# One tile for the B, c and sb rows, and the first chunk's down products ahead of the row-tile session

## What is computed

```
gate = x @ W_gate.T + 0.5 * (x @ A_gate[id].T) @ B_gate[id].T     # up: the same with its own weights
act  = silu(gate) * up                                            # 1376 columns
down = act @ W_down.T + 0.5 * (act @ A_down[id].T) @ B_down[id].T
x    = x + down @ sign(W0).T + bias0
y    = (x @ B1[id1].T) @ A1[id1].T
x    = x + y @ (W1 + 2 * sum_n w_n B_n A_n).T + bias1
```

## Time and profile before

| what | value |
|---|---|
| median of 3 runs | 875.0 us (874.68 to 875.05) |
| the profiled execution's own time | 874.75 us |
| its span | 872.9 us |
| TensorE matmuls busy | 867.7 us (99% of the span) |
| TensorE weight loads busy | 714.2 us (82%) |
| VectorE busy | 523.2 us (60%) |
| ScalarE busy | 231.5 us (27%) |
| data moved by DMA | 205.60 MB, mean 236 GB/s |
| B rows, L437 | 128 transfers, 236.0 KB each, median 3.2 us to landing |

### The profile page before, as it was taken

One profiled execution on the slowest core, in us unless ns is written; L12 is line 12 of the kernel. 1 busy time (PEld: TensorE's weight loads), 2 busy tenths in 40 slices (PEclk: granted clock), 3 DMA queues, 4 the chain that ended last, 5 costly groups with the idle time before them and its releaser, 6 DMA issues.

```text
span 872.9 us, 21554 instructions
## 1 busy us (share of the span) xinstructions
PE 867.7 (99%) x7474; PEld 714.2 (82%) x7474; DVE 523.2 (60%) x1204; ACT 231.5 (27%) x460; POOL 86.8 (10%) x122
## 2 busy tenths in 40 slices
PE   9999999999999999999999999999999999999998
PEld 6888888888888888888888888888888888888885
DVE  5797556655555566556556665655656565656654
ACT  4953212222222122212222231212122222212210
POOL 0232000000010000100000000000000000000011
PEclk9999999999999999999999999999999999999999
DMA  9967788685877767587876757688675768868563
GB/s 347 408 229 267 228 253 262 195 268 163 257 250 237 249 219 239 180 257 227 256 247 227 245 178 248 208 268 256 223 238 184 245 198 264 265 217 266 190 173 89
DMA packets 159771, 205.60 MB, mean 236 GB/s; under 512 B 56064, under 2 KB 121600, under 8 KB 152064
## 3 DMA queue, kind: packets, MB, share of 16 engines
q1 hardware_dynamic: 101536, 117.14, 43.1%
q10 hardware_dynamic: 56096, 80.76, 27.8%
q0 software_dynamic: 2112, 7.34, 2.2%
HBM read 158.76 MB, written 15.20 MB: 199 GB/s over the span
## 4 chain that ended last, share of the span: by engine, by line
PE 99%; DVE 1%; ACT 0%; issue 0%; DVEq 0%
PE gu_ps L1125 56%; PE y_ps L1230 27%; PE out_ps L1252 3%; PE gu_ps L1340 3%; PE out_ps L1303 2%; PE gu_ps L1331 1%; PE out_ps L1239 1%; PE y_ps L1125 1%; PE out_ps L1125 1%; PE gu_ps L1230 1%; PE out_ps L1260 1%; PE gu_ps L1424 0%; DVE a_lo L817 0%; PE gu_ps L1380 0%; DVE weff_raw L1032 0%; PE y_ps L1307 0%
## 5 line engine op out<-in xcount | busy, mean ns | idle before, releaser
L1230 PE MATMUL y_ps<-down_sb,actT_sb 128*128 128x512 f32 x1023 | 241.5, 393 | 0.0
L1230 PEld LDWEIGHTS y_ps<-down_sb,actT_sb 128*128 128x128 f32 x1023 | 189.6, 188 | 60.3 <-issue 21.4
L1125 PE MATMUL gu_ps<-wg_sb,xT_sb 128*128 128x432 f32 x768 | 164.0, 362 | 0.5 <-DVE act_all L835 0.5
L1125 PE MATMUL gu_ps<-wu_sb,xT_sb 128*128 128x432 f32 x768 | 160.8, 358 | 0.0
L1125 PEld LDWEIGHTS gu_ps<-wu_sb,xT_sb 128*128 128x128 f32 x768 | 144.5, 188 | 8.3
L1125 PEld LDWEIGHTS gu_ps<-wg_sb,xT_sb 128*128 128x128 f32 x768 | 141.7, 188 | 11.6 <-DVE xT_sb L817 1.4
L591 ACT CAST actT_sb<-landed 128x512 fp32r<-128x512 f32 (+1 forms) x96 | 51.1, 585 | 162.1 <-DMA landed<-act_all 89.4
L537 POOL TENSOR_TENSOR b_two<-b_raw,const_sb 128x128 f32<-128x128 f32 x62 | 24.2, 411 | 685.4 <-DMA b_raw<-in_b1tab 685.4
L1125 PE MATMUL gu_ps<-slot,s_sb 128*128 128x512 f32 x270 | 66.8, 392 | 0.0
L839 DVE STREAM_TRANSPOSE act_all<-act_all 128x512 f32<-128x512 f32 (+1 forms) x96 | 64.1, 668 | 3.3
L591 ACT COPY ad_two<-a_raw 128x352 f32<-128x352 f32 x64 | 28.0, 485 | 126.2 <-PE out_ps L1252 125.5
(11 more groups left out here) (173 smaller groups left out, 929.9 us busy)
## 6 DMA issues: line engine op xcount, KB each, us to landing
slot<-t_table ACTq DMA_DIRECT2D x59, 1024.0 KB, 8.0
b_rows<-in_btab SPq DMA_DIRECT2D x128, 236.0 KB, 3.2
a_raw<-in_atab SPq DMA_DIRECT2D x128, 152.0 KB, 8.0
landed<-act_all SPq DMA_DIRECT2D x132, 64.0 KB, 4.7
xT_raw<-in_xT SPq DMA_DIRECT2D x32, 256.0 KB, 2.6
x_in<-in_x SPq DMA_DIRECT2D x32, 256.0 KB, 10.3
landed<-act_all ACTq DMA_DIRECT2D x124, 64.0 KB, 4.7
out_x<-out_sb SPq DMA_DIRECT2D x31, 256.0 KB, 8.3
```

The lines of the kernel that those rows point to most:

```text
L1125: last = nc.tensor.matmul(o, w, m, start=start and n == 0, stop=stop and n == len(terms) - 1, skip_group_check=not check)
L1230: last = nc.tensor.matmul(to[:], actT_sb[:, ACTT_SLOT[c] + n, a, :], down_sb[:, blk, b, :], start=begin and (c, n) == (0, 0) and (a, b) == ...
```

## The change

It does four things. The tiles `b_rows` and `cs_rows` become one, `rows_sb` (2 x 944): columns 0 to 511 of groups 2 and 3 take the c and sb rows, columns 512 to 943 chunk 2's B rows. The table of B is cut in two: `btab` holds 944 columns for groups 0 and 1, `btab2` 432 columns for groups 2 and 3, and the load of a step has eight transfers in place of four, 32 partitions each (118 KB and 54 KB by their shapes). TensorE's wait for `x1_done` and `down` for chunk 0 stand ahead of the session, so `down` opens `y_ps` and the down rows add to it. The c rows of the last step get a tile `c_end` of their own, and four small tiles of the prologue get places of their own.

```diff
-                    rows, n = rows_of(b, 0, 4)
-                    sp.dma_start(b_rows[rows, n, :],
-                                 btab[bass.ds(at[b], P), :].rearrange("(q r e) w -> q r (e w)", q=4, e=2)
+                    rows, n = rows_of(b, 0, 2)
+                    sp.dma_start(rows_sb[rows, n, :],
+                                 btab[bass.ds(at[b], P), :].rearrange("(q r e) w -> q r (e w)", q=2, e=4)
+                                 ).then_inc(L["b_in"], 16)
+                for b in range(GB):
+                    rows, n = rows_of(b, 2, 4)
+                    sp.dma_start(rows_sb[rows, n, H:PAIR],
+                                 btab2[bass.ds(at[b], P), :].rearrange("(q r e) w -> q r (e w)", q=2, e=4)
                                  ).then_inc(L["b_in"], 16)
...
-            def down_rows(n, to=y_ps, begin=True):
-                return nc.tensor.matmul(to[pair(n), :], lhs_sb[group(3), pair(n)], cs_rows[group(3), n, :],
-                                        start=begin, stop=False, skip_group_check=True)
+            def down_rows(n, to=y_ps):
+                return nc.tensor.matmul(to[pair(n), :], lhs_sb[group(3), pair(n)], rows_sb[group(3), n, 0:H],
+                                        start=False, stop=False, skip_group_check=True)
...
                 if prev is not None:
                     pe.wait_ge(L["td_ready"], g)
                     pe.wait_ge(L["sbd_in"], 16 * GB * g)
-                    after(pe, L["x1_done"], prev)
...
                 gate(g, 2)
                 up(g, 2)
+                if prev is not None:
+                    after(pe, L["x1_done"], prev)
+                    down(prev, 0, begin=True).then_inc(L["y_mm"], 1)
                 lora_ready(g, j, parity, prev, pp)
                 first_rows(prev, pp)
                 second_rows()
                 if prev is not None:
-                    for c in range(NC):
+                    for c in range(1, NC):
                         down(prev, c).then_inc(L["y_mm"], 1)
```

More of the change, by code:

```diff
@@ L141, in build_adaln_ffn @@
         lhs2_sb = place("lhs2_sb", [P, P], f32)
-        rows_at = [cursor[0]]
-        b_rows = place("b_rows", [P, PAIRS, PAIR], f32)
-        cs_rows = place("cs_rows", [P, PAIRS, H], f32)
+        rows_sb = place("rows_sb", [P, PAIRS, PAIR], f32)
         rows_end = cursor[0]
@@ L178, in build_adaln_ffn @@
         const_sb = place("const_sb", [P, CONST_W], f32, line=32)
+        c_end = nc.alloc_sbuf_tensor_at("c_end", [P, PAIRS, H], f32, offset=s0_at)
+        assert s0_at + 4 * PAIRS * H <= pair_end
         b1_end = nc.alloc_sbuf_tensor_at("b1_end", [P, PAIRS, KC, 2, RANK], f32, offset=a_at)
         idx_feat = place("idx_feat", [P, 2, BATCH], i32, line=32)
+        bias0_sb = nc.alloc_sbuf_tensor_at("bias0_sb", [P, H], f32, offset=cursor[0])
+        id_raw = place("id_raw", [P, 2, BATCH], i32, line=32)
+        id_f = place("id_f", [P, 2, BATCH], f32, line=32)
+        idle_sb = nc.alloc_sbuf_tensor_at("idle_sb", [P, 512], bf16, offset=cursor[0])
+        cursor[0] += 1024
         assert cursor[0] <= nc.sbuf_usable_end, (cursor[0], nc.sbuf_usable_end)
@@ L369, in load_sbd, with load_c @@
                 rows, n = low_rows(b, 3)
-                engine.dma_start(cs_rows[rows, n, :], sb_view[bass.ds(at[b], P), :].rearrange("(r e) w -> r (e w)", e=8)
+                engine.dma_start(rows_sb[rows, n, 0:H], sb_view[bass.ds(at[b], P), :].rearrange("(r e) w -> r (e w)", e=8)
                                  ).then_inc(L["sbd_in"], 16)
-        def load_c(engine, at, batch=range(GB), to=2, signal=L["c_in"]):
+        def load_c(engine, at, batch=range(GB), to=rows_sb, r=2, signal=L["c_in"]):
             for b in batch:
-                rows, n = low_rows(b, to)
-                engine.dma_start(cs_rows[rows, n, :], c_view[bass.ds(at[b], P), :].rearrange("(r e) w -> r (e w)", e=8)
+                rows, n = low_rows(b, r)
+                engine.dma_start(to[rows, n, 0:H], c_view[bass.ds(at[b], P), :].rearrange("(r e) w -> r (e w)", e=8)
                                  ).then_inc(signal, 16)
@@ L475, in step @@
                 else:
-                    load_c(sp, table_rows(SP, 1, g), range(GB), 1, E["c_in"])
+                    load_c(sp, table_rows(SP, 1, g), range(GB), c_end, 1, E["c_in"])
                 if prev is not None:
@@ L1300, in small, with out_rows @@
                 last.then_inc(L["small_mm"], 1)
-            def out_rows(n, r=2, to=out_ps, at=slice(0, H)):
-                return nc.tensor.matmul(to[pair(n), at], lhs_sb[group(r), pair(n)], cs_rows[group(r), n, at],
+            def out_rows(n, r=2, rows=rows_sb, to=out_ps, at=slice(0, H)):
+                return nc.tensor.matmul(to[pair(n), at], lhs_sb[group(r), pair(n)], rows[group(r), n, at],
                                         start=True, stop=True, skip_group_check=True)
-            def down_rows(n, to=y_ps, begin=True):
-                return nc.tensor.matmul(to[pair(n), :], lhs_sb[group(3), pair(n)], cs_rows[group(3), n, :],
-                                        start=begin, stop=False, skip_group_check=True)
+            def down_rows(n, to=y_ps):
+                return nc.tensor.matmul(to[pair(n), :], lhs_sb[group(3), pair(n)], rows_sb[group(3), n, 0:H],
+                                        start=False, stop=False, skip_group_check=True)
             def lora_ready(g, j, parity, prev, pp):
@@ L1331, in first_rows @@
                         last = nc.tensor.matmul(gu_ps[GU_BANK[0][u]][pair(n), 0:w], lhs_sb[group(u), pair(n)],
-                                                b_rows[group(u), n, 0:w], start=False, stop=True, skip_group_check=True)
+                                                rows_sb[group(u), n, 0:w], start=False, stop=True, skip_group_check=True)
                 last.then_inc(L["first_mm"], 1)
@@ L1338, in second_rows @@
                         c, u = 1 + r // 2, r % 2
-                        lhs, w = lhs_sb if c == 1 else lhs2_sb, CHUNKS[c][1]
+                        lhs, at, w = (lhs_sb, B_SECOND, MID) if c == 1 else (lhs2_sb, H, CHUNKS[2][1])
                         last = nc.tensor.matmul(gu_ps[GU_BANK[c][u]][pair(n), 0:w], lhs[group(r), pair(n)],
-                                                b_rows[group(r), n, B_SECOND:B_SECOND + w], start=False, stop=True,
+                                                rows_sb[group(r), n, at:at + w], start=False, stop=True,
                                                 skip_group_check=True)
@@ L1396, in finish @@
                 for n in range(PAIRS):
-                    last = down_rows(n, y_end, False)
+                    last = down_rows(n, y_end)
                 last.then_inc(L["y_mm"], 1)
@@ L1417, in finish @@
                     for n in range(PAIRS):
-                        last = out_rows(n, 1, bank, columns(half))
+                        last = out_rows(n, 1, c_end, bank, columns(half))
                     last.then_inc(L["first_mm"], 1)
@@ L1512 @@
     wd[:, used] = v["L0_cond_W_down"][:, order.reshape(FP)[used]]
-    b_rows = np.zeros((R0, 4, RANK, PAIR), np.float32)
-    for u, part in enumerate((gate_b, up_b)):
-        part = part.reshape(R0, RANK, F)
-        for c, (f, w) in enumerate(CHUNKS):
-            to = 0 if c == 0 else B_SECOND
-            b_rows[:, u + (2 if c == 2 else 0), :, to:to + w] = part[:, :, f:f + w]
+    by_row = [part.reshape(R0, RANK, F) for part in (gate_b, up_b)]
+    wide, narrow = (np.stack([np.concatenate([part[:, :, CHUNKS[c][0]:sum(CHUNKS[c])] for c in cs], axis=2) for part in by_row],
+                             axis=1) for cs in ((0, 1), (2,)))
     b1_rows = v["L1_cond_B"][:, :, turned_features(0, H, KC).reshape(H)].reshape(R1, RANK, KC, P)
@@ L1528 @@
         "bd": feat(v["L0_cond_B_down"][0].transpose(1, 0, 2).reshape(H, R0 * RANK)),
-        "btab": b_rows.reshape(R0 * P, PAIR // 2),
+        "btab": wide.reshape(R0 * P, PAIR // 4),
+        "btab2": narrow.reshape(R0 * P, CHUNKS[2][1] // 4),
         "atab": np.concatenate([a_rows, ad_rows], axis=1),
```

9 lines of the change are left out of this document (3 added, 6 removed).

## The result

The changed kernel takes 877.26 us in the median of 17 executions (875.65 to 878.05), the kernel before 875.0 us in 17 on the same chip (874.68 to 875.32). The ratio is 1.0023, with an interval of 1.0017 to 1.003: 2.3 us slower, or 0.23%. The forecast was 876.1 us. The profiled execution took 876.61 us (span 874.8 us), 1.9 us over the profiled one of before.

The account below looks back on a forecast made before the run. TensorE, busy 706.00 of 706.00 us from 126 to 832 us, bounds the loop; the last step's chain leaves it. Terms 0 + 0 + 1.1 + 0 = +1.1 us gave a median of 876.1 us, range 873.9 to 879.0.

Parts of the forecast that it names:

- A: The forecast case: only the last step's tail pays, 876.1 us, within 875.4 to 877.0; chance 0.60.
- the mark for slower: Whole kernel: a median over 876.75 us counts as slower, since measurement resolves 0.2% (1.75 us); chance 0.23.
- B: Rival: in most loop pairs later act sends meet weight-table loads, making p3 or `small` late; 880.3 us with the tail; chance 0.12.
- E: Rival: B rows come late, serialized, costing 0.3 us in each odd step; 880.3 us; chance 0.04.
- The move costs nothing on TensorE: Around the session: the same 9 down matmuls run, 2.08 us, before it and not after; 0 us.
- rival D: Session entry gets cheaper, its waits met under 512-column matmuls: 0.08 us in each of 31 sessions, 873.6 us; chance 0.12.
- 2.08 us later behind the session, hidden 30 times: Work following the session shifts every step but stays covered in the loop: 0 us, at most 0.2; not hidden the 31st time.
- The B rows cost nothing: Each step's B load: eight issues fit SyncE's queue and rows land before their session; 0 us.
- E's 3.4 us of spare: SyncE's queue: slack claimed after the last B row issue before the session needs the rows, making late rows unlikely.
- The tail, +1.1 us: Last step: chunk 0's low part delays add_y and down of chunk 1; +1.1 us, bounds 0 and 2.08.
- The step that failed: Last step's end: `low_rank_rows` follows down of chunk 1 and x1's landing, moved 1.04 us; the chain behind keeps 1.1.

Follow-up runs that it names:

- fillers: Changed kernel plus five filler matmuls in TensorE's gap of the last step, between the down products of steps 30 and 31: 877.6 us, ratio 1.0023.
- last two steps: Kernel before, with chunk 0's down products ahead of the session in steps 30 and 31 only: 876.18 us, ratio 1.0012.
- two chunks ahead: Kernel before, with chunks 0 and 1 of down (21 matmuls) ahead of the session in step 31 only: 881.26 us, ratio 1.0072.
- The swap: Changed kernel, with ScalarE's two sends of x1 put ahead of its two sb row loads in the last step: 876.43 us, ratio 1.0017.
- the move alone: Kernel before, with chunk 0's nine down matmuls ahead of the session, old tiles and four B transfers kept: 876.56 us, ratio 1.0024.
- the tables alone: Changed kernel with its tiles and split tables, but down wholly behind the session as before: 875.03 us, ratio 1.0003.
- step 31 alone: Kernel before, with chunk 0's nine down matmuls ahead of the session only in the last step: 875.82 us, ratio 1.0012.

## Why the spare of x1 was gone

ScalarE and its queue in the last step: before, changed, and changed with fillers (the long execution); of each the cast of chunk 1, the sb rows and the sends of x1.

```profile
855.26 0.62 ACT L591 CAST actT_sb<-landed 128x512 fp32r<-128x512 f32 x1 [0.93 <-DMA landed<-act_all]
855.81 0.88 ACTq L370 DMA_DIRECT2D cs_rows<-sb_table  x2
857.42 1.47 ACTq L350 DMA_DIRECT2D x_landed<-x_turn  x2
```

```profile
858.25 0.62 ACT L598 CAST actT_sb<-landed 128x512 fp32r<-128x512 f32 x1 [1.07 <-DMA landed<-act_all]
858.71 0.80 ACTq L372 DMA_DIRECT2D rows_sb<-sb_table  x2
859.55 1.36 ACTq L352 DMA_DIRECT2D x_landed<-x_turn  x2
```

```profile
857.98 0.62 ACT L598 CAST actT_sb<-landed 128x512 fp32r<-128x512 f32 x1 [1.33 <-DMA landed<-act_all]
858.58 1.01 ACTq L372 DMA_DIRECT2D rows_sb<-sb_table  x2
859.63 1.45 ACTq L352 DMA_DIRECT2D x_landed<-x_turn  x2
```

Before, the queue is idle from 856.69 to 857.42 and waits for the transpose of x1. After the change it is never idle: the sends follow the sb rows at once (859.51, 859.55), since the cast of chunk 1 ahead of them moved by 2.99 us and the transpose by 1.72 (0.99 us of both had been lost before the last session). From the end of these sends to `low_rank_rows`' turn on TensorE (the end of the matmuls ahead of it) it is 861.03 - 858.89 = 2.14 us before, 862.92 - 860.91 = 2.01 after, and 857.39 + 5.00 - 861.08 = 1.31 in the long execution. In the first two the last of these sends lands 0.5 to 0.6 us before that turn, in the third 1.2 us after it.

The 0.7 us between 2.01 and 1.31 would by themselves have made it late by 0.2 us. The other 1.0 us is the landing, which takes longer there. These are the second send of x1 on ScalarE's queue and the load of x on SyncE's, in the low and in the long execution:

```profile
860.14 0.77 ACTq L352 DMA_DIRECT2D x_landed<-x_turn  x1
860.65 0.59 SPq L465 DMA_DIRECT2D x_in<-in_x  x1
```

```profile
860.19 0.60 SPq L465 DMA_DIRECT2D x_in<-in_x  x1
860.29 0.79 ACTq L352 DMA_DIRECT2D x_landed<-x_turn  x1
```

In the low one the send (64 KB) is issued 0.5 us ahead of the load (256 KB) and lands in 2.26 us; in the long one it is issued 0.1 us behind the load and takes 3.30 us, and lands 0.3 us after the load does. All 14 profiles split this way: in 11 the send goes first, by 0.18 to 0.95 us, and takes 2.14 to 2.40 us; in three (fillers, last two steps, two chunks ahead) it goes 0.1 us behind, and takes 3.30 to 3.36. So a send that is late by a few tenths lands a whole us later, which fits an upper and a lower group of executions. No run moved the load of x to test this.

The few tenths come from chunk 1. Its cast starts 9.07 to 9.19 us behind the first matmul of the last session in those three profiles, and 8.68 to 8.90 in the others, but for two: that with chunk 0's sends shared, which has another order, and that with the old order in the last step. There it starts 9.22 us behind, as late as in the long ones, and the sends of x1 go out right behind the transpose all the same.

So the transfer had only some 0.5 us of spare before the change either. What the change took away is the idle time in front of its sends, which had absorbed a late chunk 1.

## The prediction, point by point

- *The time.* The forecast was +1.1 us and +2.3 came. 877.26 us is over 877.0, the upper end of what A allows, and over 876.75, the mark for slower, which had 0.23. It lies within 873.9 to 879.0 because that range reached up for B and E, whose waits in the loop did not come. That part is luck.
- *The move costs nothing on TensorE.* Right: 11.85 us from `up` to the next `gate` in both. The session's entry did not become cheaper (rival D), its idle time rose from 0.29 to 0.35 us.
- *2.08 us later behind the session, hidden 30 times.* Right in kind: no wait of TensorE in the loop ends with `landed`, `x_landed` or s_sb. With the last step in the old order 0.7 us over the kernel before are left, with an interval that includes none. The swap leaves 1.5 - 0.9 = 0.6 us beside chunk 0's part, which agrees. The profiles show part of it: from the session of step 2 to that of step 31 it is 729.13 us before, and 0.1 to 0.5 us more than that and the move in the profiles of the move alone (0.11), of the old last step (0.47) and of the changed kernel without the wait for the B rows (0.27 and 0.49). In step 5 of the first profile the wait adds 0.7. What makes the small pieces was not settled.
- *The B rows cost nothing.* Right for the tables alone. With the move one session in one execution lost 0.7 us (E's mechanism, once and not in each odd step). E's 3.4 us of spare is 445.0 - 441.6, counted from the landing and not, as its words have it, from the last issue; from there it is 445.0 - 439.0 = 6.0 by the prediction and 6.15 as measured. A set of issues that took 1.4 us longer does not use that up: in step 5 the session was ready 4.3 us after the last issue ended, so those rows must have landed late as well, some 5 us after it.
- *The tail, +1.1 us.* The path, chunk 0's low part in front of add_y and of `down`, is the one that the chain shows, and its size was nearly right: 0.91 us in the profile, 0.9 us for step 31 alone, for a forecast of 1.1. The 13 executions of the changed kernel under 877 have a median of 876.24, close to the forecast; since that holds some tenths from the loop, the match is partly chance.
- *The step that failed* is "`low_rank_rows` at 861.03 follows them and x1's landing, which moved 1.04; everything behind is a chain and keeps the 1.1". It took the sends of x1 to hang on add_y alone. On ScalarE they also stand behind the cast of chunk 1, which moved by 2.0 us against the stretch before, and the sb rows; so they lost their idle time, and in 20 of 33 executions x1 seems to be late by 1.2 to 1.4 us. The sum did not have that wait. B had its kind, later sends that meet loads and land later, but in the loop, with the loads of the weight tables, and not in the last step. The swap and the two profiles with the wait show that it makes long executions; in a profiled execution of the changed kernel itself it was never caught, so for that kernel it is inferred.

The sum by the runs: 0.9 us fixed for chunk 0's low part, 0.6 to 0.7 us from the loop (0.1 to 0.5 of it seen in profiles, its cause open), and the rest, some 0.7 to 0.8 us of the median, from executions with x1 late. The profiles put an execution into one or the other group by whether the last send of x1 is issued before or after SyncE's load of x; why chunk 1 lands a few tenths later in some executions is open.

## What to carry to other kernels

When work is moved in a step that repeats, price the last repetition by itself, and for each transfer in it list everything that stands ahead of its issue on that engine, casts that wait for another landing among them, and not only what makes its data. An idle time of a queue in front of a send is spare; a shift that closes it shows first as scatter between executions and only then in a profile. Where two queues issue at nearly the same time, look at which goes first: here 0.1 us behind a large load went with a landing 1 us later. And when the median lies above the profiled execution, look for profiles of the long ones before explaining the short one.

## What the hardware showed unexpectedly

- The clock: 3.83 us without a matmul, and the granted clock fell to 0.50 in the stretch behind it (21 matmuls in 6.65 us, not 5.10). After 0.84 to 1.44 us without one in the last step of the other profiles it stayed at 1.00.
- Sends issued 2 us later land sooner: act from SyncE's queue takes a median of 2.5 us to landing after the change and 4.7 before. It is 2.7 with the move alone and 4.7 with the tables alone, so the move does it; with the slot loads 3 us later it is 3.2. What else they no longer collide with was not tried.
- A send of 64 KB that was issued 0.1 us behind a load of 256 KB on the other queue took 3.30 to 3.36 us to landing (3 profiles), and one issued ahead of it 2.14 to 2.40 (11 profiles).
- Four issues of 54 KB take 2.53 us, four of 118 KB 2.58 us, and four of 236 KB 2.56 us: these issues cost 0.64 us each whatever they carry, and one set of four took 3.96 us. Others cost less: that of xT, 256 KB, takes 0.36 us.
